# Cross-attention's V product as seven half-size products a batch in a perceiver layer on one Trainium2 core

## The reference

```python
q = x @ Wq + bq                       # x: layernorm of [32, 32, 512]
kv = context @ Wkv + bkv              # context: [32, 257, 512]
k, v = jnp.split(kv, 2, axis=-1)      # 16 heads of 32
q = _larope(q, Lq); k = _larope(k, Lk)
scores = jnp.einsum('bhqd,bhkd->bhqk', q, k) * SCALE
attn = jax.nn.softmax(masked(scores), axis=-1)
out = jnp.einsum('bhqk,bhkd->bhqd', attn, v)
return out.reshape(B, Lq, H * hd) @ Wo + bo
```

## Time and profile before

| | |
|---|---|
| median of 3 runs | 789.95 us (lowest 788.63) |
| span of the profiled execution | 792.4 us |
| share of that span in which PE had work | 97% |
| the same for DVE, ACT, POOL | 62%, 43%, 27% |
| cross-attention (from the first product to the last `attend`) | about 5 to 548 us |
| one tile of four batches in it | 66.0 us |

### The profile page before, as it was taken

How to read it: one execution, slowest core, us unless ns; L and a number is a source line. 1 busy time by engine, 2 the same in 40 slices (tenths; PEclk the granted TensorE clock), 3 DMA queues, 4 the chain that set the end, 5 groups by cost and what they waited for, 6 DMA issues and landing times. The chain is left out here.

```text
span 792.4 us, 21581 instructions
## 1 busy us (share of the span) xinstructions
PE 768.4 (97%) x9062; PEld 648.3 (82%) x9063; DVE 489.8 (62%) x1129; ACT 341.0 (43%) x816; POOL 216.6 (27%) x192
## 2 busy tenths in 40 slices
PE   8999999999999999999999999999899999599997
PEld 7888888888888888888888888887677777478784
DVE  6656575565655557556565655856879998722136
ACT  5533534335343353433534335443566664133330
POOL 1222223222232222322223222231123321246640
PEclk9999999999999999999999999999899999789999
DMA  8722001001010001100001001201933237634448
GB/s 295 277 82 81 29 28 55 28 28 30 28 55 28 29 28 29 55 28 28 30 29 55 28 28 30 81 28 55 370 153 147 104 121 303 234 120 163 169 135 317
DMA packets 22445, 78.11 MB, mean 99 GB/s; under 512 B 3248, under 2 KB 3760, under 8 KB 19408
## 3 DMA queue, kind: packets, MB, share of 16 engines
q1 hardware_dynamic: 18672, 64.71, 22.6%
q0 software_dynamic: 3680, 12.06, 4.5%
HBM read 58.15 MB, written 18.61 MB: 97 GB/s over the span
## 5 line engine op out<-in xcount | busy, mean ns | idle before, releaser
L161 PE MATMUL bank<-chi,wparts 128*128 128x258 f32 x496 | 143.7, 290 | 0.0
L163 PE MATMUL bank<-chi,wparts 128*128 128x258 f32 x496 | 140.1, 282 | 0.0
L162 PE MATMUL bank<-clo,wparts 128*128 128x258 f32 x496 | 140.0, 282 | 0.0
L334 POOL TENSOR_TENSOR pdiag_hi<-p_last_and_rinv_hi,const 128x256 fp32r<-128x256 f32 x32 | 19.8, 618 | 328.5 <-DVE p_last_and_rinv_hi L581 328.5
L328 POOL TENSOR_TENSOR ksin<-kb,const 128x1032 f32<-128x1032 f32 x32 | 95.0, 2968 | 40.0 <-ACT kb L381 40.0
L786 PE MATMUL bank<-wparts,chi 128*128 128x512 f32 x256 | 105.8, 413 | 0.0
L161 PEld LDWEIGHTS bank<-chi,wparts 128*128 128x128 f32 x496 | 93.5, 188 | 12.8 <-issue 12.8
L787 PE MATMUL bank<-wparts,chi 128*128 128x512 f32 x256 | 101.3, 396 | 0.0
L788 PE MATMUL bank<-wparts,clo 128*128 128x512 f32 x256 | 101.1, 395 | 0.0
L373 ACT ACTIVATE chi<-craw 128x1032 fp32r<-128x1032 f32 x32 | 34.3, 1071 | 146.6 <-PE bank L788 144.1
L557 DVE TENSOR_TENSOR v<-bank,bias_cross 128x512 f32<-128x512 f32 x64 | 43.9, 688 | 83.9 <-PE bank L788 83.9
(11 more groups left out here) (326 smaller groups left out, 1684.6 us busy)
## 6 DMA issues: line engine op xcount, KB each, us to landing
craw<-ctx_t_dram SPq DMA_DIRECT2D x32, 516.0 KB, 3.5
expert_lo<-weights_dram SPq DMA_DIRECT2D x8, 1024.0 KB, 13.1
expert_hi_scratch<-wraw SPq DMA_DIRECT2D x16, 512.0 KB, 2.8
wparts<-expert_hi_scratch SPq DMA_DIRECT2D x8, 1024.0 KB, 8.8
wraw<-weights_dram SPq DMA_DIRECT2D x7, 1024.0 KB, 5.9
expert_lo<-ffn_out_scratch SPq DMA_DIRECT2D x16, 256.0 KB, 5.7
x<-x_dram SPq DMA_DIRECT2D x8, 256.0 KB, 7.9
ffn_xn_scratch<-xn SPq DMA_DIRECT2D x8, 256.0 KB, 2.9
```

The costliest lines, as they stand in the source:

```text
L161: pe.matmul(psum, ahi(c), bhi(c), start=(c == 0), stop=False)
L162: pe.matmul(psum, ahi(c), blo(c), start=False, stop=False)
L163: last = pe.matmul(psum, alo(c), bhi(c), start=False, stop=(c == chunks - 1))
```

## The change

V of rows 0 to 255 of the context is a 256 x 512 by 512 x 512 product. It is cut into 2 x 2 blocks of rows, inner dimension and columns, and computed by Strassen's scheme in Winograd's form: seven products of 128 x 256 by 256 x 256, six matmuls each of 256 columns, in place of eight. They are called V_1 to V_7 here after the scheme, and come in the order V_1, V_2, V_5, V_6, V_3, V_7, V_4. The parts of it:

- GpSimd forms four differences of the context's blocks for each batch (`ctx_sums`, three instructions: one of 512 and two of 256 elements a partition), ScalarE rounds them (`ctx_sums_hi`, 1024 elements), VectorE makes the lo part (`ctx_sums_lo`, 1024 elements). For the weights the same once, at the start (`wv_sums`, `wv_sums_hi`, `wv_sums_lo`). Batch 0 is computed with eight products, of 256 columns (`first_v_product`).
- Products are summed in PSUM where the scheme allows, and copied out on the way: ScalarE makes four copies of 256 columns a batch (`v_first_evac` after V_1, `v_fifth_evac` after V_5, `v_sum_evac` after V_6, `v_21_evac` after V_4), VectorE three sums of 256 columns (`v_11`, `v_12`, `v_22`) in place of two `v_evac` of 512. The bias of V is added after attention, by GpSimd (`o_bias`, between `o_sum` and `o_hi`).
- TensorE's step is now: scores; V_1, V_2; K products 0 and 1; V_5, V_6; transposes; K product 2; V_3, V_7; K product 3; the extra; V_4; diagonals; attend. K products 1 to 3 all use one bank.
- `k_sin` is cut in two halves, the second behind evacuation 3; `ctx_sums` stands between diagonals and that half.
- The layernorm's scaling moves from VectorE to ScalarE (`ln_apply`, by a factor and a shift that GpSimd makes in `ln_shift`), behind the copies of the probabilities and ahead of evacuations 2 and 3. The output bias is added to x by GpSimd (`x_bias`) in j=1.
- To make room, the mask is loaded in eight parts of four batches instead of two parts, masked scores are written straight to `pr`, `qcos`/`qsin` share memory with `pr`, and `last_raw` with `v`. A small difference on `last_raw` stands before `q_rope` in VectorE's start.

The diff, cut to its core:

```diff
             def _(pool):
+                def ctx_sums(b, j):
+                    raw = craw[j % 2]
+                    pool.wait_ge(s_ctx[j % 2], (b // 2 + 1) * 16)
+                    if b > 1:
+                        pool.wait_ge(s_tlo, b - 1)
+                    pool.tensor_tensor(traw[:, T1:T3 + 1, :, :], raw[:, :, P:2 * P].rearrange("p (i c) n -> p i c n", i=2),
+                                       raw[:, 0:2, 0:2 * P].rearrange("p c (h n) -> p h c n", h=2), ALU.subtract).then_inc(s_tr, 1)
...
+                        if b > 0:
+                            o_bias(b - 1)
+                        if more:
+                            k_sin(b + 1, 0)
                         diagonals(b)
                         if j == 0:
                             ln_pool(pool, t + 1)
-                        if not (last and j == BT - 1):
-                            k_sin(b + 1)
+                            ln_shift(t + 1)
+                        if not (last and j >= BT - 2):
+                            ctx_sums(b + 2, j)
+                        if more:
+                            k_sin(b + 1, 1)
+                        if j == 1:
+                            if t == 0:
+                                pool.wait_ge(s_bo, 16)
+                            x_bias(t)
...
             def _(act):
+                        if more:
+                            v_first_evac(b + 1, j + 1)
                         exp(b, 0)
                         exp(b, 1)
                         if more:
                             k_evac(b + 1, 0)
                         exp(b, 2)
                         exp(b, 3)
...
+                        if more:
+                            k_evac(b + 1, 1)
+                        if not begin and more:
+                            v_fifth_evac(b + 1, j + 1)
+                            v_sum_evac(b + 1, j + 1)
+                        if not begin:
                             o_hi(b - 1, t if j > 0 else t - 1, (j + BT - 1) % BT)
...
+                        for g in range(G):
+                            pt_evac(b, g)
+                        if j == 0:
+                            ln_apply(t + 1, x[:, 0 if last else t + 1, :])
+                        if more:
                             k_evac(b + 1, 2)
                             k_evac(b + 1, 3)
...
+                        if more:
+                            v_21_evac(b + 1, j + 1)
+                        if not (last and j >= BT - 2):
+                            ctx_sums_hi(b + 2)
...
             def _(dve):
                         for g in range(G):
                             masked(b, j, g)
-                        if not (first and j == 0):
+                        if more:
+                            v_11(b + 1, j + 1)
+                        if not begin:
                             o_sum(b - 1)
                         inverse_sums(b)
                         pair_parts(b)
...
+                        if j == 0:
+                            ln_stats(t + 1, x[:, 0 if last else t + 1, :])
                         if not (last and j >= BT - 2):
                             ctx_lo(b + 2, j)
-                        if j == 0:
-                            ln(t + 1, x[:, 0 if last else t + 1, :])
...
+                        elif more:
+                            v_12(b + 1, j + 1)
+                            v_22(b + 1, j + 1)
                             k_cos(b + 1)
...
-                        if more:
-                            v_evac(b + 1, j + 1, 1)
+                        if not (last and j >= BT - 2):
+                            ctx_sums_lo(b + 2)
...
             def _(pe):
+                def v_product(psum, rows, block, start):
+                    (hi, lo), (whi_i, wlo_i) = rows, wv_block(block)
+                    for c in range(2):
+                        pe.matmul(psum, hi[:, c, :], whi_i[:, c, :], start=start and c == 0, stop=False, skip_group_check=not start)
+                        pe.matmul(psum, hi[:, c, :], wlo_i[:, c, :], start=False, stop=False, skip_group_check=not start)
+                        last = pe.matmul(psum, lo[:, c, :], whi_i[:, c, :], start=False, stop=c == 1, skip_group_check=not start)
+                    return last
...
                         scores(b, j)
                         if more:
-                            for m in range(4):
-                                k_product(b + 1, j + 1, m)
+                            v_first_two(b + 1, j + 1)
+                            k_product(b + 1, j + 1, 0)
+                            k_product(b + 1, j + 1, 1)
+                            if not begin:
+                                v_next_two(b + 1)
...
                         probs_transposed(b)
                         if more:
-                            v_product(b + 1, j + 1, 0)
+                            k_product(b + 1, j + 1, 2)
+                            if not begin:
+                                v_third_and_seventh(b + 1, j + 1)
+                            k_product(b + 1, j + 1, 3)
...
-                        if more:
-                            v_product(b + 1, j + 1, 1)
+                        if more and not begin:
+                            v_fourth(b + 1)
                         diagonals_spread(b)
                         attend(b, j)
```

More of the change, by code:

```diff
@@ L192, in perceiver @@
             clo = [sb(f"clo{i}", [P, KC, LKP], F32R) for i in range(2)]
-            last_raw = sb("last_raw", [P, KC, B])
-            last_parts = sb("last_parts", [P, KC, 2 * B], F32R)
+            sv_hi = sb("wv_sums_hi", [P, 3, D], F32R)
+            sv_lo = sb("wv_sums_lo", [P, 3, D], F32R)
+            traw = sb("ctx_sums", [P, 4, 2, P])
+            thi = sb("ctx_sums_hi", [P, 4, 2, P], F32R)
+            tlo = sb("ctx_sums_lo", [P, 4, 2, P], F32R)
             kb = sb("kb", [P, 4, LKP])
@@ new lines, in perceiver, with product_of, copy_of, sum_of @@
+            L_DIFF, L_HI, L_LO, L_PRODUCT, L_COPY, L_SUM = range(1, 7)
+            def product_of(b, k):
+                return 2 + 7 * (b - 1) + k
+            def copy_of(b, k):
+                return 4 * (b - 1) + k
+            def sum_of(b, k):
+                return 2 + 3 * (b - 1) + k
+            WV_PARTS = 2 * KC - 1
+            WV_SUMS = 4
+            V_1, V_2, V_5, V_6, V_3, V_7, V_4 = range(1, 8)
+            C_P1, C_P5, C_U2, C_21 = range(1, 5)
+            S_11, S_12, S_22 = range(1, 4)
@@ new lines, in o_bias, with x_bias, ln_shift @@
+                def o_bias(b):
+                    pool.wait_ge(s_onorm, b + 1)
+                    pool.tensor_tensor(onorm[:], onorm[:], bias_cols[:, 4:4 + G].unsqueeze(2).to_broadcast([P, G, S]),
+                                       ALU.add).then_inc(s_obias, 1)
+                def x_bias(t):
+                    pool.wait_ge(s_xn, t + 1)
+                    pool.tensor_tensor(x[:, t, :], x[:, t, :], bias[:, R_BO, :], ALU.add).then_inc(s_xb, 1)
+                def ln_shift(n):
+                    pool.wait_ge(s_rstd, n + 1)
+                    pool.tensor_scalar(shift[:], mv[:, 0:1], rstd[:, 0:1], -1.0, ALU.mult, ALU.mult).then_inc(s_shift, 1)
@@ L342, in _ @@
                 pool.tensor_copy(same[:], const[:, C_SAME:C_SAME + P]).then_inc(s_same, 1)
-                k_sin(0)
+                k_sin(0, 0)
+                k_sin(0, 1)
+                wv_sums()
+                ctx_sums(1, 1)
                 def body(t, last=False):
@@ L347, in body @@
                         b = t * BT + j
+                        more = not (last and j == BT - 1)
+                        if b > 0:
+                            o_bias(b - 1)
+                        if more:
+                            k_sin(b + 1, 0)
                         diagonals(b)
@@ L358, in _ @@
                 ln_pool(pool, TILES + 1)
+                o_bias(B - 1)
             @block.scalar
@@ new lines, in v_sum_evac, with v_21_evac, ln_apply @@
+                def v_sum_evac(b, j):
+                    act.wait_ge(s_vp1, product_of(b, V_6))
+                    act.activation(v[j % 2][:, 1, 0:HALF], v_base, ACT.Copy).then_inc(s_va, 1)
+                def v_21_evac(b, j):
+                    act.wait_ge(s_vp1, product_of(b, V_4))
+                    act.activation(v[j % 2][:, 0, HALF:D], v_base, ACT.Copy).then_inc(s_va, 1)
+                def ln_apply(n, xt):
+                    act.wait_ge(s_shift, n)
+                    act.wait_ge(s_xtp, n)
+                    act.activation(xn[:], xt, ACT.Identity, bias=shift[:, 0:1], scale=rstd[:, 0:1]).then_inc(s_xn, 1)
@@ L483, in body @@
                             w_hi(AQ)
+                        if last and j == 2:
+                            w_hi(AK)
                         if j == 1:
@@ L676, in body @@
                             w_lo(AK)
-                        if more:
-                            v_evac(b + 1, j + 1, 0)
-                        if j == 0 and first:
-                            v_last()
```

(1 more changed line is left out.)

371 lines of the change are left out of this document (254 added, 117 removed).

## The result

The changed kernel takes 817.9 us (median of four, 816.2 to 819.5), against 789.3 for the kernel before beside it: ratio 1.037 with a 95% interval of 1.035 to 1.039, 28.6 us more. One of the four executions of before took 1480.9 us; the other three lie between 788.5 and 790.0. Run again later, beside other kernels, the changed kernel took 821.2 against 789.7 (1.040, 1.038 to 1.043). The forecast was 801, with 782 to 813.

A forecast was written before the change was run, and what follows sets the result against it. TensorE was taken to bound the kernel, busy 97%. Saving -16.7, batch 0 +0.2, loop waits +21.0, start +6.5 and end +0.4 gave +11.4 us on 792.4: 803.8 profiled, 801 as median, range 782 to 813.

The forecast's parts named there:

- The saving on TensorE: V in the loop: 42 matmuls of 256 columns replace 24 of 512, saving 0.54 us a batch, 16.7 in all.
- Rival E: V matmuls: a fixed cost in each of the 42 costs 31 us, total 821; chance 0.03.
- The wait before the scores of j=1 and j=3: After K product 3, TensorE waits for k_sin, 0.8 us in j=1 and 0.4 in j=3.
- q_rope into the sum parts: VectorE's q_rope and ctx_sums_lo delay masks and v_11, so K product 1 waits 0.4 us in j=3.
- LayerNorm on ScalarE: In j=0, ln_apply delays K evacuation 2, so K product 3 waits 1.2 us.
- Sum of the loop: Loop waits total 2.8 us a tile, 21.0 over 7.5 tiles; bounds 0.85 (6.4) and 3.1 (23.3).
- The start: Before the first scores: late last_raw, VectorE and GpSimd turns, and ScalarE roundings cost 2.5 to 9 us, 6.5 taken.
- the first masks: Sign in the start: masks of batch 0 begin at 30 to 34 us, 27.73 before.
- C: Loop: ScalarE's copies come late for bank 1 in each batch, slower by over 2%, 816 us; chance 0.15.
- B: Loop and start: GpSimd and VectorE hardly hinder each other, waits 6.4 us, start 1.5, total 782; chance 0.20.
- D: Whole kernel: all waits hidden and start neutral, faster by over 2%, 773.5 us; chance 0.05.
- the tile: Sign in the loop: a cross-attention tile takes 66.0 + 0.6 us.

The follow-up runs named there:

- b1: The kernel before, with each of its eight V products in two halves of 256 columns: 793.2 us, 1.004 of before.
- e7: The changed kernel, with VectorE's ctx_sums_lo moved from the end of a step to behind v_11 of the next step: 816.1 us.
- e1: The changed kernel, with ScalarE's ln_apply placed behind K evacuations 2 and 3 and not ahead of them: 805.9 us.
- e9: The changed kernel with ln_apply behind evacuations 2 and 3, k_cos halved, wv_sums behind first q, first-step K copy 1 before roundings, ctx_sums_lo behind next v_11: 785.3 us.
- e5: The changed kernel, with GpSimd's wv_sums waiting until VectorE has read the first q out of PSUM: 815.3 us.
- e2: The changed kernel, with VectorE's k_cos cut in two halves, the first started after K evacuations 0 and 1: 813.6 us.
- e4: The changed kernel, with GpSimd's ctx_sums left out from batch 2 on, three one-element subtractions in their place: 821.1 us.

## Why the prediction was wrong, point by point

That the kernel gets slower, the mechanisms in the loop and their places were right. Two terms of the sum failed. The waits of the loop were put at 21.0 us, at most 23.3, and the loop came out 10.2 us longer than that gives; the start was put at 6.5, at most 9, and scores 1 came 11.7 us later in one run and 16.2 in the other. Neither bound held. The points below say what was short in each.

- **The saving on TensorE: right.** Steps without a wait show it alone: j=2 went from 17.58 to 17.00, and j=0 with its wait taken away from 17.57 to 17.00. That is 0.57 a batch; 0.54 was forecast. Rival E is out by b1.
- **The wait before the scores of j=1 and j=3: the term for handing over was mis-sized.** Forecast 0.8 and 0.4. Timelines of PE, ACT, DVE and POOL, after, end of a j=1 step (207.21 is the last matmul of K product 3):

```profile
207.21 0.28 PE L165 MATMUL bank<-chi,wparts 128*128 128x258 f32 x1
207.53 0.48 ACT L494 ACTIVATE kb<-bank,bias_cols 128x258 f32<-128x258 f32 x1 [2.40 <-PE bank L165]
208.04 1.23 DVE L733 TENSOR_TENSOR kcos<-kb,const 128x1032 f32<-128x1032 f32 x1 [1.53 <-ACT kb L494]
208.09 2.24 POOL L385 TENSOR_TENSOR ksin<-kb,const 128x516 f32<-128x516 f32 x1 [0.45 <-ACT kb L494]
```

  Of the forecast chain 0.20 + 0.51 + 1.15 + 1.10 + 0.05 = 3.01 all terms but the last stand: k_sin ends at 210.33, 3.00 after the product's end at 207.33. Then TensorE started at 210.58: 0.25, not 0.05. The term of 0.05 for handing k_sin to TensorE was short by 0.2. So 3.25 of work against the forecast 2.20 (j=1) and 2.64 (j=3) of room: 1.05 and 0.61, measured 1.02 and 0.58.
- **q_rope into the sum parts: right in kind, 0.4 forecast.** The trace shows 0.28 idle, e7 gave 0.56 back. The profile counts idle time from the end of the last record (0.28 long) and the next start would have come 0.12 after the last, so a wait inside a run of matmuls costs some 0.16 more than it is shown as. The first matmul after such a wait also took 0.23 to the next start and not 0.12 (96.92 to 97.15): 0.28 + 0.16 + 0.11 = 0.55.
- **LayerNorm on ScalarE: right in kind, 1.2 forecast, 1.80 measured by e1.** Timelines of DVE, POOL, ACT and PE, after, from the scores' start at 243.84:

```profile
253.27 1.23 DVE L686 TENSOR_TENSOR clo<-craw,chi 128x1032 fp32r<-128x1032 f32 x1
253.43 1.47 POOL L183 TENSOR_TENSOR rstd<-vareps,neghalf 128x1 f32<-128x1 f32 x1 [0.61 <-DVE vareps L179]
255.29 0.81 ACT L588 ACTIVATE xn<-x,neg_mean_rstd,rstd 128x512 f32<-128x512 f32 x1 [2.03 <-POOL neg_mean_rstd L425]
256.01 0.46 ACT L494 ACTIVATE kb<-bank,bias_cols 128x258 f32<-128x258 f32 x1
256.52 0.39 PE L163 MATMUL bank<-chi,wparts 128*128 128x258 f32 x1 [1.53 <-ACT kb L494]
```

  rstd starts at +9.59 (forecast 9.6) and lets `clo` pass (1.47 for 0.55), ln_apply at +11.45 (11.0 to 11.5), evacuation 2 at +12.17 (12.2), product due at +10.99 (11.03). The failing step: I let the product start with the evacuation. It starts 0.51 after, when the copy of 0.46 has ended: 1.69 late, and 1.80 with the 0.11 of the first matmul after a wait.
- **Sum of the loop.** Waits of 1.02 in j=1, 1.09 in j=3 (16.26 less the 15.17 of e9) and 1.80 in j=0 make 3.9 us a tile, not 2.8: 8.3 us over 7.5 tiles. A wait of tile 0 was left out (`w_lo(WO)` on VectorE ahead of `ctx_sums_lo`): 1.6 by e7. The loop was forecast at -0.54 x 30 + 21.0 = +4.8 and measured at +15.0; these two are 9.9 of the 10.2 between.
- **The start: 6.5 forecast.** Scores 0 came 7.0 later and the first masks at 34.66, the 34 of strict turns. What failed was to take one number between two bounds where the terms come one after the other, and bounds that left two terms out. The roundings ahead of copy 1 (up to 2.9 in the text) cost 2.6 on top, the layernorm's chain another 2.2 to 2.7 in step 0, where it has longer lo parts ahead of it: a wait that the prediction had only for the loop. The clock cost up to 3.4 more: 11.7 to scores 1 in one run, 16.2 in the other. No term of the prediction had the clock in it.
- **Rivals.** C, whose number is nearest (816), is not what happened: evacuation 2 waits only in j=0, ScalarE's copies of V never hold TensorE, and where e1 moved nothing but ln_apply the waits on ScalarE went. B (782) is refuted by e5 and e2, D by each tile. That GpSimd's differences are hidden was right (e4). That C's number is near is luck. Of the signs that the prediction named, the first masks (34.66, sign 30 to 34) and the tile (67.8, sign 66.6) also came out beyond what it said.

The Trainium skill (SBUF — State Buffer, "SBUF: two separate sides") has the shared ports as a lock held for the whole instruction. The rows above agree: a power of one element a partition took 1.47 behind a VectorE instruction, and the 0.42 of `qswap` became 1.48.

## What to carry to other kernels

When a change shortens the way between two dependent stages, add up that way with every handover in it, from the start of the last matmul to the start of the next consumer. Between the end of one engine's row and the start of the next engine's lay 0.03 us (ScalarE to VectorE), 0.05 (ScalarE to TensorE) and 0.25 (GpSimd to TensorE) here; ScalarE's copy started 0.32 after the last matmul had, and each copy of a K product stands in the way with its own 0.46 to 0.48. Then look for what stands ahead of a critical copy only by the order of the queue: moving one instruction (e1) gave 12 us, five edits together turned a loss of 28.6 us into a gain of 4 (e9).

## What the hardware showed that I had not expected

- VectorE with two SBUF operands and GpSimd took strict turns over a whole chain: four instructions of 0.42 took 1.37 to 1.48 each, one GpSimd instruction between any two.
- Waits of 2 to 6 us were followed by a granted clock of 0.50 in some stretches and 1.00 in others of the same program: one first step of 24.6 us, another of 28.6. In b1 the clock stood at 0.50 from 42 to 46 us though TensorE had been busy since 26.0.
- A further matmul in a dense run costs 6 ns beside its columns (b1), so splitting columns is nearly free at 256.
